# A LayerNorm pass with a new order inside each round, and three loads and one projection moved between the stages of an attention and LoRA block

## The reference

```python
xn = _layernorm(x, axis=-1)
x = x + _L0_attn_ref(xn, w_qkv, w_o) + _L0_ffn_ref(xn, gate, kernel, bias, lora_A, lora_B, lora_A_shared, lora_B_shared)
```

## Time and profile before

| | us |
|---|---|
| time, median of 3 runs | 5074.66 |
| lowest, highest | 5000.89, 5322.9 |
| the profiled execution's own time | 4991.53 |
| its span (slowest core, first to last instruction) | 4990.0 |
| spans of the eight cores | 4929.0 to 4990.0 |

### The profile page before, as it was taken

One profiled execution on the slowest core, in us unless ns is written; L12 is line 12 of the kernel. 1 busy time (PEld: TensorE's weight loads), 2 busy tenths in 40 slices (PEclk: granted clock), 3 DMA queues, 4 the chain that ended last, 5 costly groups with the idle time before them and its releaser, 6 DMA issues.

```text
span 4990.0 us, 42989 instructions; the slowest of 8 cores (4929.0 to 4990.0 us)
## 1 busy us (share of the span) xinstructions
PE 4026.7 (81%) x16144; PEld 1531.2 (31%) x16144; DVE 1070.1 (21%) x1490; ACT 947.0 (19%) x849; POOL 511.7 (10%) x790
## 2 busy tenths in 40 slices
PE   2222999679986999888888888888886999569999
PEld 0000444234432444222222222222222444223343
DVE  2344222101101222122112222211220000011222
ACT  2222000000000000444444444444440000000000
POOL 0000000000000000222222222222220000000000
PEclk8666999889998999888889888888988999789999
DMA  9997232342327664111111111111117443467653
GB/s 147 169 172 171 88 119 87 79 115 87 97 68 122 97 93 73 37 31 38 34 34 32 38 32 30 38 33 35 32 30 111 89 87 69 96 125 151 143 132 102
DMA packets 419978, 419.67 MB, mean 84 GB/s; under 512 B 60352, under 2 KB 380096, under 8 KB 419392
## 3 DMA queue, kind: packets, MB, share of 16 engines
q0 software_dynamic: 212352, 223.93, 27.0%
q1 hardware_dynamic: 207424, 192.98, 12.7%
HBM read 495.46 MB, written 83.89 MB: 116 GB/s over the span
## 4 chain that ended last, share of the span: by engine, by line
PE 71%; DMA 12%; DVE 9%; another core or an unknown queue 4%; ACT 1%; issue 1%; SPq 0%; DVEq 0%; POOL 0%; ACTq 0%; POOLq 0%
PE kv_p L86 17%; PE a_rw L81 12%; PE a_av L86 9%; PE w_p L86 9%; PE q_p L86 9%; DMA f_at<-sc_at 5%; PE a_s L86 5%; DVE a_rc L81 4%; PE f_p L86 4%; PE a_s L81 4%; DMA lkv_x<-xTkv 3%; DMA sc_xkv<-lkv_o 2%; DVE f_s L81 2%; PE f_pl L86 1%
## 5 line engine op out<-in xcount | busy, mean ns | idle before, releaser
L81 ACT ACTIVATE a_p<-a_s,p_btab 128x1024 bf16<-128x1024 f32 x768 | 815.7, 1111 | 2457.6 <-PE a_s L81 2456.3
L86 PE MATMUL a_av<-a_p,a_v 128*128 128x512 bf16 x1536 | 601.5, 392 | 0.0
L81 PE MATMUL a_rw<-a_p,p_onesb 128*1 128x512 bf16 x1536 | 584.2, 380 | 0.0
L86 PE MATMUL f_p<-f_k,f_x 128*128 128x512 bf16 x2048 | 466.3, 387 | 70.1 <-DMA f_bs<-bsT 42.7
L86 PE MATMUL kv_p<-kv_w,kv_x 128*128 128x512 bf16 x1984 | 440.5, 380 | 82.6 <-DMA kv_w<-wvT 82.6
L86 PE MATMUL q_p<-q_x,q_w 128*128 128x512 bf16 x1984 | 440.5, 380 | 64.7 <-DMA q_x<-sc_xkv 64.7
L86 PE MATMUL kv_p<-kv_x,kv_w 128*128 128x512 bf16 x1984 | 441.5, 381 | 45.3 <-DMA kv_x<-sc_xkv 45.3
L86 PE MATMUL w_p<-w_w,p_attn 128*128 128x512 bf16 x1984 | 440.6, 380 | 41.4 <-DMA w_w<-woT 41.4
L81 DVE TENSOR_TENSOR a_p<-a_p,p_cm 128x512 bf16<-128x512 bf16 x256 | 97.5, 422 | 1174.1 <-ACT a_p L81 1174.1
L86 PE MATMUL a_s<-a_q,a_k 128*128 128x512 bf16 x768 | 323.0, 421 | 30.0 <-ACT a_p L81 16.1
L81 PE MATMUL lkv_ps<-lkv_x,p_onesb 128*1 128x512 bf16 x256 | 108.7, 425 | 263.8 <-ACT lkv_q L81 263.4
(11 more groups left out here) (91 smaller groups left out, 2050.5 us busy)
## 6 DMA issues: line engine op xcount, KB each, us to landing
kv_x<-sc_xkv SPq DMA_DIRECT2D x16, 4096.0 KB, 14.1
lkv_x<-xTkv POOLq DMA_DIRECT2D x8, 4096.0 KB, 42.7
sc_xkv<-lkv_o SPq DMA_DIRECT2D x64, 512.0 KB, 3.9
q_w<-wqT POOLq DMA_DIRECT2D x16, 2048.0 KB, 16.3
w_w<-woT POOLq DMA_DIRECT2D x8, 4096.0 KB, 26.5
f_k<-kern POOLq DMA_DIRECT2D x8, 4096.0 KB, 31.5
a_k<-sc_k POOLq DMA_DIRECT2D x384, 64.0 KB, 2.2
a_v<-sc_v POOLq DMA_DIRECT2D x192, 128.0 KB, 2.8
```

What stands on the lines that cost most here:

```text
L81: getattr(eng, m)(*aa, **kk).then_inc(s, st)
L86: getattr(eng, m)(*aa, **kk)
```

## The change

- `ln_pass`: two inner functions. A round tc runs the hook, `do_stats(tc)`, then `do_xprime(tc - 1)`, then issues the load of tc+1, which waits for the last x' multiply and for all stores of chunk tc-1; `do_xprime(7)` follows the loop. Slabs are two feature blocks, 16 of them instead of eight, in statistics and x'. The multiply writes back into the chunk buffer, and the 256 KB store reads from there; the staging tiles are gone. The copied sums have two sets.
- `kv_sweeps`: the tables of rotation are loaded at its start, behind the barrier.
- `lora_pre`: the LoRA projection is a stage of its own ahead of attention, with its own load of xq; its results stay in `sb_axg`, `sb_axs`. The final phase loads xq again, and bias and blocks at once.
- `attention`: loads the mask itself. The first Wo block is issued by GpSimd behind its last attention load, and the barrier does not wait for it (`gd_front`).

```diff
-    def barrier():
-        for r in (pe, ve, ac, gd):
+    def barrier(gd_front=None, sy_front=None):
+        for r in (pe, ve, ac):
             for sem, v in r.frontier():
                 sy.wait(sem, v)
-        for sem, v in sy.frontier():
+        for sem, v in (gd_front if gd_front is not None else gd.frontier()):
+            sy.wait(sem, v)
+        for sem, v in (sy_front if sy_front is not None else sy.frontier()):
             sy.wait(sem, v)
...
-            sq = [pp(nc.sbuf_tensor(f"l{tag}_q{i}", [128, SLAB], BF16)) for i in range(2)]
-            tb = [pp(nc.sbuf_tensor(f"l{tag}_t{i}", [128, SLAB], BF16)) for i in range(2)]
-            ob = [pp(nc.sbuf_tensor(f"l{tag}_o{i}", [128, SLAB], BF16)) for i in range(2)]
...
+            sq = [pp(nc.sbuf_tensor(f"l{tag}_q{i}", [128, 2 * CH], BF16)) for i in range(2)]
+            tb = [pp(nc.sbuf_tensor(f"l{tag}_t{i}", [128, 2 * CH], BF16)) for i in range(2)]
...
-            for tc in range(nch):
...
+            def do_stats(tc):
...
-                for sl in range(8):
+                for sl in range(16):
                     si = sl % 2
                     ac.waitd(xload[xi])
                     ac.wait(s_pe, qdep[si])
                     av = ac.call("activation", sq[si][:],
-                                 xch[xi][:, sl * SLAB:(sl + 1) * SLAB], AF.Square)
+                                 xch[xi][:, sl * 2 * CH:(sl + 1) * 2 * CH], AF.Square)
                     pe.wait(s_ac, av)
-                    for k in range(4):
-                        dc = 4 * sl + k
+                    for k in range(2):
+                        dc = 2 * sl + k
...
+                stats_done[tc] = pe.ctr.v
+                ve.wait(s_pe, stats_done[tc])
                 ve.wait(s_ve, ve.ctr.v)
...
+                ve.call("tensor_copy", srow[ri][0:1, :], p_sum[0:1, :])
+                row_done = ve.call("tensor_copy", qrow[ri][0:1, :], p_sq[0:1, :])
+
+            def do_xprime(tc):
...
-                for sl in range(8):
+                stores = []
+                for sl in range(16):
                     ti = sl % 2
                     ve.wait(s_ve, tdep[ti])
...
-                    ve.waitd(odep[ti])
                     ve.wait(s_ve, v1)
                     v2 = ve.call("tensor_mul",
-                                 ob[ti][:].rearrange("p (a t) -> p a t", a=4),
-                                 tb[ti][:].rearrange("p (a t) -> p a t", a=4), bcr_b)
+                                 xs.rearrange("p (a t) -> p a t", a=2),
+                                 tb[ti][:].rearrange("p (a t) -> p a t", a=2), bcr_b)
                     tdep[ti] = v2
                     last_tt = v2
                     sy.wait(s_ve, v2)
...
                 xfree[xi] = last_tt
+                xstore[xi] = stores
+
+            gd.wait(s_ve, xfree[0])
+            xload[0] = gd.dma(out=xch[0][:].rearrange("p (a t) -> p a t", a=32),
+                              in_=fview(xT_in)[:, :, 0:CH])
+            for tc in range(nch):
+                if hook is not None:
+                    hook(tc)
+                do_stats(tc)
+                if tc > 0:
+                    do_xprime(tc - 1)
+                if tc + 1 < nch:
+                    ni = (tc + 1) % 2
+                    gd.wait(s_ve, xfree[ni])
+                    gd.waitd(xstore[ni])
+                    xload[ni] = gd.dma(
+                        out=xch[ni][:].rearrange("p (a t) -> p a t", a=32),
+                        in_=fview(xT_in)[:, :, (tc + 1) * CH:(tc + 2) * CH])
+            do_xprime(nch - 1)
...
+            wk_deps = wk_deps + [gd.dma(out=cosb[:], in_=i_cos_kv),
+                                 gd.dma(out=sinb[:], in_=i_sin_kv)]
...
+    def lora_pre():
...
+            xv = [sy.dma(out=xq[:].rearrange("p (a t) -> p a t", a=32)[:, :, 0:CH],
+                         in_=fview(sc_xkv)[:, :, 3 * CH:4 * CH]),
...
+            lg = [gd.dma(out=aall[:].rearrange("p (a r) -> p a r", a=32),
+                         in_=fview(i_aall)),
...
+            pe.waitd(xv)
+            pe.waitd(lg)
+            for nt in range(4):
+                for tc in range(2):
+                    for dc in range(32):
...
+    lora_pre()
+    barrier()
...
+                cmld = gd.dma(out=sb_cm4[:], in_=i_cm4)
+                ve.waitd(cmld)
...
         attention()
-        barrier()
-
-        def wo_phase():
+        gdf = gd.frontier()
+        gv0 = gd.dma(out=wo[0][:].rearrange("p (a o) -> p a o", a=32),
+                     in_=fview(i_woT)[:, :, 0:CH])
+        barrier(gd_front=gdf)
...
-                lg = [gd.dma(out=aall[:].rearrange("p (a r) -> p a r", a=32),
-                             in_=fview(i_aall)),
...
-                pe.waitd(xv)
-                pe.waitd(lg)
...
+            pe.waitd(xv)
             bias = pp(nc.sbuf_tensor("f_bias", [128, D], F32))
```

More of the change, by code:

```diff
@@ L231, in ln_pass @@
             xfree = [0, 0]
+            xstore = [None, None]
             qdep = [0, 0]
             tdep = [0, 0]
-            odep = [None, None]
             row_done = 0
-            gd.wait(s_ve, xfree[0])
-            xload[0] = gd.dma(out=xch[0][:].rearrange("p (a t) -> p a t", a=32),
-                              in_=fview(xT_in)[:, :, 0:CH])
-            for tc in range(nch):
+            stats_done = {}
+            def do_stats(tc):
+                nonlocal row_done
                 xi = tc % 2
[L241 to L248, removed]
+                ri = tc % 2
                 pe.waitd(xload[xi])
                 pe.wait(s_ve, row_done)
-                for sl in range(8):
+                for sl in range(16):
                     si = sl % 2
@@ L317, in ln_pass @@
                     sy.wait(s_ve, v2)
[L318 to L320 removed]
+                    stores.append(sy.dma(
+                        out=fview(sc_out)[:, 2 * sl:2 * sl + 2, tc * CH:(tc + 1) * CH],
+                        in_=xs.rearrange("p (a t) -> p a t", a=2)))
                 xfree[xi] = last_tt
+                xstore[xi] = stores
[16 more added lines that the diff above has]
+            do_xprime(nch - 1)
     def rope_block(b0, b1, cs, sn, bufs, dst0, dst1):
@@ L440, in build_program @@
         wsb = plk(nc.sbuf_tensor("kv_w", [128, 32 * KVH * HD], BF16))
[L441 to L444, removed]
+        wk_deps = []
         def wk_hook(tc):
@@ L518, in build_program @@
     barrier()
+    def lora_pre():
+        with ExitStack() as ps:
+            pp = ps.enter_context
+            xq = pp(nc.sbuf_tensor("lp_x", [128, 32 * TOWN], BF16))
+            aall = pp(nc.sbuf_tensor("lp_aall", [128, 32 * NRTOT], BF16))
+            asb = pp(nc.sbuf_tensor("lp_as", [128, 32 * RANK], BF16))
+            pl = pp(nc.psum_tensor("lp_pl", [128, CH], F32))
+            pls = pp(nc.psum_tensor("lp_pls", [RANK, CH], F32))
+            xv = [sy.dma(out=xq[:].rearrange("p (a t) -> p a t", a=32)[:, :, 0:CH],
+                         in_=fview(sc_xkv)[:, :, 3 * CH:4 * CH]),
+                  sy.dma(out=xq[:].rearrange("p (a t) -> p a t", a=32)[:, :, CH:2 * CH],
+                         in_=fview(sc_xkv)[:, :, 7 * CH:8 * CH])]
+            lg = [gd.dma(out=aall[:].rearrange("p (a r) -> p a r", a=32),
+                         in_=fview(i_aall)),
+                  gd.dma(out=asb[:].rearrange("p (a r) -> p a r", a=32),
+                         in_=fview(i_asT))]
+            pe.waitd(xv)
[3 more added lines that the diff above has]
+                    for dc in range(32):
+                        pe.call("matmul", pl[:],
+                                aall[:, dc * NRTOT + nt * 128:dc * NRTOT + (nt + 1) * 128],
+                                xq[:, dc * TOWN + tc * CH:dc * TOWN + (tc + 1) * CH],
+                                start=(dc == 0), stop=(dc == 31), inc=(dc == 31))
+                    pv = pe.ctr.v
+                    ve.wait(s_pe, pv)
+                    vv = ve.call("tensor_scalar",
+                                 sb_axg[:, nt * TOWN + tc * CH:nt * TOWN + (tc + 1) * CH],
+                                 pl[:], sb_gnr[:, tc * 4 + nt:tc * 4 + nt + 1], None,
+                                 ALU.mult)
+                    pe.wait(s_ve, vv)
+            for tc in range(2):
+                for dc in range(32):
+                    pe.call("matmul", pls[:],
+                            asb[:, dc * RANK:(dc + 1) * RANK],
+                            xq[:, dc * TOWN + tc * CH:dc * TOWN + (tc + 1) * CH],
+                            start=(dc == 0), stop=(dc == 31), inc=(dc == 31))
+                pv = pe.ctr.v
+                ve.wait(s_pe, pv)
+                vv = ve.call("tensor_copy", sb_axs[:, tc * CH:(tc + 1) * CH], pls[:])
+                pe.wait(s_ve, vv)
@@ L522, in build_program @@
         sb_attn = pp(nc.sbuf_tensor("p_attn", [128, NH * TOWN], BF16))
+        wo = [pp(nc.sbuf_tensor(f"w_w{i}", [128, 32 * CH], BF16)) for i in range(2)]
         def attention():
@@ L694, in wo_phase @@
                 sdep = [None, None]
[L695 to L697 removed]
```

(1 more changed line is left out.)

88 lines of the change are left out of this document (28 added, 60 removed).

## The result

The changed kernel is slower: 5253.18 us at the median of 10 runs (5246.63 to 5444.89) against 5037.77 for the kernel before, measured beside it (10 runs, 4984.76 to 5423.92). In some executions of either kernel one half of the chip, or both, ran at a lower clock and the time was some per cent longer; compared without these, the ratio is 1.0527, 95% interval 1.0498 to 1.0556. The profiled execution has a span of 5263.3 us where the one before had 4990.0. Both slowest cores are core 1, so stages can be set side by side.

What follows compares the result with a forecast made beforehand. Transfers bound the LayerNorm; after it TensorE is busy, and its idle time counts at stage borders. LayerNorm +206, tables +9, LoRA +37 and Wo -36 gave +216 on 4991.5, so 5207.5, forecast 5215 us; range 5130 to 5340.

Steps and rivals of the forecast that it cites:

- final wait: Final phase: one wait for xq, bias and first kernel block before the final product, 80 us, ends 71 and 100.
- tables: K rotation tables, loaded behind the LayerNorm's barrier, lengthen the wait for the first K matmul: +9 us, ends 0 and +20.
- Wo prefetch: First Wo block, issued before attention ends, cuts TensorE's wait before Wo: -36 us, ends -41 and -28; second block hidden.
- Serial rounds: LayerNorm: load, statistics, row chain, x' and last store add up, 88 us a round against 54.8; +206 us; chance 0.86.
- load L: LayerNorm chunk load, no stores beside it but a 1 MB wk piece behind: 32 us, ends 25.9 and 42.7.
- Start of the stage: LayerNorm: chunks 0 and 1 load at once with 1 MB of wk between; chunk 1 is there at 76 us.
- LoRA stage: Own stage between barriers ahead of attention: wait 65.1 plus projection 81.3, +146.4 us; net +37 with the final phase.
- (a): LayerNorm: cast load lands like a plain one, 14.1 us, once stores are gone; total 5082, within 2%; chance 0.04.
- (b): LayerNorm: the next chunk's load still runs under statistics and x'; total 4967, no change; chance 0.03.
- (c): LayerNorm: TensorE stays at lower clock (+7 a round), half slabs cost 27 (+5), load 42.7 (+11); 5345; chance 0.07.

## Why the prediction was right, point by point

The sum said +216 and the two spans differ by +273. The 57 us between them are 24 in the LayerNorm, 16 in the final wait, 3 in the tables and 17 that the sum left out, less 3 in the Wo prefetch. Nearly all errors point the same way, so the forecast did not come near by errors that cancel.

**Serial rounds.** Right in mechanism and nearly in size. A round is 91.4 us where 88 was forecast. Its parts, from the round that loads at 135.97 and the six loads: load 35.9 in the mean (forecast 32); statistics from 175.16 to 196.70, 21.5 (22 and 0.5); row chain to 205.01, 8.3 (8.3); x' until the last multiply ends at 227.45, 22.4 (22); last store and restart to 230.63, 3.2 (3). The straight line through the widths 512 and 2048 gave 0.69 us for a product of 1024, and 0.69 it was.

**The load L** is the term that was mis-sized: 3.9 us times six is 23 of the 24 us by which the stage ends after 688.5. I took it nearer to the Wo blocks (25.9 to 26.5) than to the loads of the same stage (40.1 to 42.7), because stores slow the latter. The runs show two things between a Wo block and such a load. One is the 1 MB piece behind, 3 to 4 us; the prediction named it, but took 32 for a whole megabyte behind where its own row with half a megabyte stood at 31.5. The other was not in it at all: the load of the neighbouring core at nearly the same moment. A row of the same stage had both in it: the first two chunks came at 139 GB/s, and 4.2 × 10^6 bytes at that rate are 30 us, with the wk piece 38. The nearer row was the one in time, not the one in shape.

**Start of the stage.** Chunk 1's statistics were forecast for 76 and began at 79.96.

**Tables.** +12 for +9: the first K matmul came 32.4 us after the barrier.

**LoRA stage.** +146.1 for +146.4. The wait and the work were copied from rows of the same code, and they moved unchanged.

**The final wait.** The second mis-sized term, 95 for 80. The estimate reckoned 71 us for the needed bytes and 93 for all, and leant to the first. (Its own bytes and rate, 19.4 × 10^6 at 215 GB/s, give 90 for all.) It was the last: bytes queued behind the needed ones took their full share, as the run that held them back shows. In the step's words, the kernel block "queued behind" should have been counted as ahead.

**Wo prefetch.** -39.1 for -36, and the second block was hidden as said.

**The rivals.** The quick load (a) did not come: in the changed kernel no chunk load landed under 31.7 us on any core. The overlap (b) did not survive. Of (c) a part came true, in L: TensorE's clock did not stay low through the statistics. Windows of the changed kernel, core 1, the first stretch and the rest of one chunk's statistics:

```profile
175.00:181.60 6.60, 5.24 (x13) 1.53 (x14) 0.00 (x0) 4.11 (x4) 0.00 (x0) 0.50 0.20 38
181.70:196.30 14.60, 12.58 (x52) 3.52 (x50) 0.00 (x0) 12.10 (x12) 0.00 (x0) 1.00 0.00 0
```

After an idle stretch TensorE is granted 0.50, its 1.2 GHz level, for 6.6 us and 1.00, the 2.4 GHz level, for the rest. Before, 8.6 us at 0.56 came out about the same, so the longer idle time of the new order made nothing worse here.

**What the sum left out** is +17 us in the V and Q starts and in the final loop, where the code did not change. The V and Q waits were 82.3 and 64.4 before; over all cores of the kernels profiled here where nothing was held back, they lie between 75 and 85 and between 56 and 74. Such pieces move by some us from one execution to the next, and no term of the change is needed for them. What moves them was not looked for.

## What to carry to other kernels

With two buffers, write down for each wait what is still left to do while the awaited load flies. Here the answer was nothing, since the work on the full buffer stood, in VectorE's plan, behind the statistics of the empty one; moving it back ahead of them was worth 39 us in each of six rounds, and no size of slab or staging buffer mattered beside it. Removing a visible wait (VectorE's 142.6 us for stores) gains nothing when it lies beside a longer chain. And at a stage's start hold back whatever the first instruction does not need: the blocks behind it cost 27 us in one place. Last, look at more than the slowest core: one core's loads said that the piece behind them cost 1 to 2 us, and the eight together showed 3 to 4 and a second cause.

## What the runs showed of the hardware that was not expected

A 4096 KB load with a cast to bfloat16, alone on the queues of its core, took 24 to 26 us late in the program, where the neighbouring core issued its own some 20 us apart from it, and 34.3 in the LayerNorm when both issued theirs within 1 us of each other. The same load in the same stage took 26.1 once the two were 12 us or more apart. With 1 MB queued behind it, it took 38.0 at under 1 us and 31.7 at 7 to 10. The tensor and the idleness of the core account for nothing that was seen. Over the 384 loads of the eight kernels with the serial order, a straight-line fit with a step for the piece (2.6 us) gives 0.74 us less for each us of distance to the neighbour's load, and under 0.02 for each us to any other core's. It is a correlation in traces, with no run made for it.

Two loads of 4096 KB without a cast, behind a barrier and with half a megabyte of other blocks beside them, were there after 37.69 us, 223 GB/s.
